# Bias terms as c·max(d, τ): one VectorE pass for each, summed by GpSimd and VectorE, with ScalarE taking the k, v and q copies

## The reference

```
hbias   = relu(dist[..., None] @ Wth + bth)        # 32 hidden values for each (query, key) pair
qs_bias = (hbias @ Wto + bto)[..., 0]
logits  = einsum('btnh,bfnh->bnft', k, q) + bias + qs_bias[:, None]
w       = softmax(logits)
```

## Time and profile before

| | |
|---|---|
| runs | 1380.3, 1382.73, 1384.69 us; median 1382.73 |
| profiled execution | 1388.81 us; its span, first to last instruction, 1387.1 us |
| groups 1 to 15's bias sums end | 125.1 to 1131.3 us |
| busy PE, DVE, ACT, POOL | 1228.3, 1222.8, 1064.8, 834.8 us |
| granted TensorE clock, mean | 0.970 |

### The profile page before, as it was taken

How to read it: one execution, slowest core, us unless ns; L and a number is a source line. 1 busy time by engine, 2 the same in 40 slices (tenths; PEclk the granted TensorE clock), 3 DMA queues, 4 the chain that set the end, 5 groups by cost and what they waited for, 6 DMA issues and landing times.

```text
span 1387.1 us, 39817 instructions
## 1 busy us (share of the span) xinstructions
PE 1228.3 (89%) x11184; PEld 1013.8 (73%) x11184; DVE 1222.8 (88%) x4922; ACT 1064.8 (77%) x3353; POOL 834.8 (60%) x889
## 2 busy tenths in 40 slices
PE   1599989898989899898989898989898999788897
PEld 1377878787878787777878787878787878666665
DVE  4899989898989999898989898989898988579996
ACT  4588878787878888787878686878787876568886
POOL 3677767676767677676767676767676754211110
PEclk9899999999999999999999999999999999989999
DMA  5201000002110000021100101111101000000000
GB/s 153 67 7 30 16 27 12 29 12 76 44 31 12 23 19 22 20 68 34 31 25 13 29 12 31 57 47 28 31 12 42 12 12 9 5 22 19 18 20 9
DMA packets 69117, 41.06 MB, mean 30 GB/s; under 512 B 14841, under 2 KB 63873, under 8 KB 68993
## 3 DMA queue, kind: packets, MB, share of 16 engines
q1 hardware_dynamic: 68992, 39.84, 10.1%
HBM read 23.29 MB, written 1.05 MB: 18 GB/s over the span
## 4 chain that ended last, share of the span: by engine, by line
issue 27%; DVE 24%; ACT 18%; PE 17%; POOL 3%; DVEq 1%; DMA 1%; ACTq 0%; SPq 0%; POOLq 0%
ACT prob L802 10%; DVE bias_acc L951 4%; PE M L582 3%; ACT relu_z L785 3%; PE O L552 3%; DVE score L998 3%; DVE qT L1123 3%; DVE hid L1073 3%; DVE st L1016 2%; PE M L628 2%; PE M L560 2%; PE L L689 1%; ACT probT L809 1%; ACT oT L814 1%; DVE rs L1025 1%
## 5 line engine op out<-in xcount | busy, mean ns | idle before, releaser
L802 ACT ACTIVATE prob<-score,nmax 128x128 f32<-128x128 f32 x1024 | 396.7, 390 | 182.7 <-DVE nmax L998 177.3
L1396 POOL TENSOR_TENSOR prob<-prob,rinv 128x512 f32<-128x512 f32 x256 | 293.9, 1148 | 234.0 <-DVE rinv L1006 231.9
L951 DVE SCALAR_TENSOR_TENSOR bias_acc<-relu_z,cst,bias_acc 128x512 f32<-128x512 f32 x370 | 339.7, 918 | 9.7 <-ACT relu_z L785 0.2
L785 ACT ACTIVATE relu_z<-dist_g,cst 128x512 f32<-128x512 f32 x386 | 294.9, 804 | 16.9 <-DMA cst<-cst_all 16.9
L998 DVE CUSTOM_DVE_ANT_0 score<-L,bias 128x128 f32<-128x128 f32 x1024 | 233.8, 282 | 4.2 <-PE L L528 1.5
L802 ACT ACTIVATION_READ_ACCUMULATOR prob<-score,nmax 128x1 f32 x1024 | 193.2, 189 | 0.0
L1391 POOL TENSOR_TENSOR sd<-mv,half 128x1 f32<-128x1 f32 x128 | 105.6, 825 | 120.4 <-DVE mv L1018 117.6
L538 PE MATMUL T<-ident,prob 128*128 128x128 f32 x1024 | 163.9, 284 | 4.7 <-POOL prob L1396 3.8
L552 PEld LDWEIGHTS O<-probT,v 128*64 128x64 f32 x2048 | 109.3, 136 | 62.0 <-issue 54.4
L582 PE MATMUL M<-wv,ctxT 128*128 128x512 f32 x256 | 147.0, 658 | 7.7 <-DVE hid L1073 5.1
L528 PE MATMUL L<-kT,qT 64*128 64x128 f32 x2048 | 149.6, 286 | 0.0
(11 more groups left out here) (134 smaller groups left out, 2226.7 us busy)
## 6 DMA issues: line engine op xcount, KB each, us to landing
dist_g<-in_fside_BxSxS SPq DMA_DIRECT2D x16, 256.0 KB, 2.7
mask_g<-in_mask_Bx1x1xS_ff SPq DMA_DIRECT2D x16, 256.0 KB, 3.5
ctxT<-ctxT_all SPq DMA_DIRECT2D x64, 64.0 KB, 1.9
xs<-x_all SPq DMA_DIRECT2D x64, 64.0 KB, 1.8
x_all<-xs SPq DMA_DIRECT2D x64, 64.0 KB, 1.9
wk<-in_L_xattn_Wk SPq DMA_DIRECT2D x4, 512.0 KB, 3.7
wv<-in_L_xattn_Wv SPq DMA_DIRECT2D x4, 512.0 KB, 4.3
wq<-in_L_xattn_Wq SPq DMA_DIRECT2D x4, 512.0 KB, 5.0
```

Source lines behind the costliest of these rows:

```text
L785: nc.scalar.activation(relu_z[:, z_slot(g, k), :], dist_g[:, :, :], ACT.Relu, bias=cst[:, C_BTH + k:C_BTH + k + 1], scale=cst[:, C_WTH + k ...
L802: last = nc.scalar.activation(prob[:, c, m, :], score[:, c, m, :], ACT.Exp, bias=nmax[:, c, m:m + 1], scale=-1.0, accum_out=rsum[:, c, m:m ...
L951: vec.scalar_tensor_tensor(out=bias_acc[:, :], in0=relu_z[:, z_slot(g, k), :], scalar=weight, in1=bias_acc[:, :], op0=ALU.mult, op1=ALU.ad ...
L1396: gp.tensor_tensor(prob[:, c, :, :], prob[:, c, :, :], rinv[:, c, :].rearrange("p (m o) -> p m o", o=1).broadcast_to([P, 4, P]), ALU.mult) ...
```

## The change

For Wth[k] not 0, relu(Wth·d + bth)·Wto is |Wth|·Wto·max(d, τ), with τ = -bth/Wth, plus a part that is linear in d. So a term is c·max(d, τ), one TENSOR_SCALAR with (max, mult), and all the linear parts together are a·1 + b·d, one TENSOR_SCALAR more.

For groups 1 to 15 (the bias of group 0 keeps the old form): DVE forms all 32 maxima into eight slots of `relu_z` (`maximum`) and begins `bias_acc` with a + b·d (`begin_sum`); POOL adds 20 of the 32 to `pool_acc`, with one instruction each (`add_term` of POOL), and its products and clamps go; DVE adds 12 to `bias_acc` as plain TENSOR_TENSORs. ACT's relus go, and ACT makes all six k, v, q copies of a unit. τ and c of all layers are computed once at the start by 23 small DVE instructions (`kinks`). SP loads one slice of constants for a group (`hst`) in place of three of `cst`.

The core of the diff (the first `add_term` is DVE's, the second POOL's):

```
+Z_SLOTS = 8
-Z_PLAN = plan([[1, 2, 2, 1, 0], [1, 2, 2, 1, 0], [1, 2, 2, 1, 0], [2, 2, 2, 0, 0]])
-TERM_PLAN = plan([[0, 2, 1, 1, 1], [1, 2, 1, 1, 1], [1, 2, 1, 1, 1], [1, 2, 2, 1, 1]])
+VEC_SLOTS = (1, 4, 6)
+VEC_TERMS = [k for k in range(BIAS_K) if k % Z_SLOTS in VEC_SLOTS]
+POOL_TERMS = [k for k in range(BIAS_K) if k % Z_SLOTS not in VEC_SLOTS]
+MAX_PLAN = plan([[0, 3, 2, 2, 1], [2, 2, 1, 2, 1], [2, 2, 1, 2, 1], [3, 3, 2, 0, 0]])
+VEC_ADD_PLAN = plan([[0, 0, 1, 1, 1], [0, 1, 1, 0, 1], [0, 1, 0, 1, 1], [1, 1, 1, 0, 0]])
+POOL_ADD_PLAN = plan([[0, 2, 2], [1, 2, 2], [1, 2, 2], [2, 2, 2]])
...
+            def maximum(g, k):
+                j = k - Z_SLOTS
...
+                vec.tensor_scalar(relu_z[:, k % Z_SLOTS, :], dist_g[:, :, :], hst[:, H_TAU + k:H_TAU + k + 1],
+                                  hst[:, H_C + k:H_C + k + 1], ALU.max, ALU.mult).then_inc(z_done, 1)
+            def begin_sum(g):
...
+                vec.tensor_scalar(bias_acc[:, :], dist_g[:, :, :], hst[:, H_B:H_B + 1], hst[:, H_A:H_A + 1], ALU.mult,
+                                  ALU.add).then_inc(term_done, 1)
+            def add_term(g, n):
...
+                vec.tensor_tensor(bias_acc[:, :], bias_acc[:, :], relu_z[:, k % Z_SLOTS, :], ALU.add).then_inc(term_done, 1)
...
             def terms(g, i, q):
...
+                    if i == 0 and q == 1:
+                        begin_sum(g + 1)
+                    for k in MAX_PLAN[i][q] if i < GROUP else ():
+                        maximum(g + 1, k)
+                    for n in VEC_ADD_PLAN[i][q] if i < GROUP else ():
+                        add_term(g + 1, n)
...
+            def add_term(g, n):
...
+                k = POOL_TERMS[n]
+                pool.wait_ge(z_done, z_count(g, k + 1))
...
+                gp.tensor_tensor(pool_acc[:, :, :], so_far[:, :, :], relu_z[:, k % Z_SLOTS, :].rearrange("p (b t) -> p b t", b=GROUP),
+                                 ALU.add).then_inc(pool_sum, 1)
...
-                if nxt:
-                    dve.wait_ge(v_done, after(g, i + 1, 2, 1))
-                    wait(dve, pv_done, after(g, i - 1, 2, 1))
-                    vec.tensor_copy(v[:, (i + 1) % 2, 512:1024], M0[:, :]).then_inc(v_kept[1], 1)
...
+                if nxt:
+                    act.wait_ge(v_done, after(g, i + 1, 2, 1))
+                    wait(act, pv_done, after(g, i - 1, 2, 1))
+                    nc.scalar.activation(v[:, (i + 1) % 2, 512:1024], M0[:, :], copy).then_inc(v_kept[1], 1)
```

More of the change, by code:

```diff
@@ L69, with z_count, wait, wait_first @@
 STATS_TERMS = (4, 8)
+def z_count(g, k):
+    return k if isinstance(g, int) and g == 0 else g * BIAS_K + (START_VEC_K - BIAS_K + k)
 def vec_count(g, k):
[L74 removed]
+    return k if isinstance(g, int) and g == 0 else g * (1 + VEC_ADDS) + (START_VEC_K - 1 - VEC_ADDS + k)
 def pool_count(g, k):
[L79 to L83 removed]
+    first = POOL_K - START_POOL_SKIP
+    return k - START_POOL_SKIP if isinstance(g, int) and g == 0 else g * POOL_ADDS + (first - POOL_ADDS + k)
 C_WTH, C_BTH, C_WTO = 0, BIAS_K, 2 * BIAS_K
 C_BTO = 3 * BIAS_K
[L89 to L90 removed]
+C_HI, C_LO, C_PW, C_PB, C_TAU, C_C = [C_BTO + 1 + n * BIAS_K for n in range(6)]
+C_A, C_B = C_C + BIAS_K, C_C + BIAS_K + 1
+C_ALL = C_B + 1
+H_TAU, H_C, H_A, H_B = [c - C_TAU for c in (C_TAU, C_C, C_A, C_B)]
+KINK_MAX = 1.0e38
+FLAT_BELOW = 1.0e-30
+E_HEADS = 16
+E_HD = 8
+EXPERTS = 8
+ROW_HEADS = 4
+F_GROUPS = BATCHES // GROUP
+VA = 32
+def wait(eng, sem, value):
+    if isinstance(value, int) and value < 1:
+        return
+    eng.wait_ge(sem, value)
+def wait_first(eng, consts, *counts):
+    pairs = [(s, v) for s, v in zip(counts[::2], counts[1::2]) if not isinstance(v, int) or v > 0]
+    pairs = [(s, v if isinstance(v, int) else eng.to_reg(v)) for s, v in pairs]
+    eng.wait_ge(consts, 3)
+    for s, v in pairs:
+        eng.wait_ge(s, v)
+def after(g, i, per, k=0):
+    return g * (GROUP * per) + (i * per + k + 1)
+CST_STEPS = 27
 E_HEADS = 16
@@ L831, in step @@
                     nc.scalar.activation(kT[:, (i + 1) % 2, 0:4, :], M0[:, :], copy).then_inc(k_kept[0], 1)
-                relus(g, i, 0)
+                relus(i, 0)
                 if cur:
                     exps(g, i, 0)
-                relus(g, i, 1)
+                relus(i, 1)
+                if nxt:
+                    act.wait_ge(k_done, after(g, i + 1, 2, 1))
+                    wait(act, qk_done, after(g, i - 1, 4, 3))
+                    nc.scalar.activation(kT[:, (i + 1) % 2, 4:8, :], M0[:, :], copy).then_inc(k_kept[1], 1)
                 if nxt:
@@ L853, in step @@
                     nc.scalar.activation(qT[:, (i + 1) % 2, 0:4, :], M0[:, :], copy, scale=HD ** -0.5).then_inc(q_kept[0], 1)
-                relus(g, i, 4)
+                    act.wait_ge(q_done, after(g, i + 1, 2, 1))
+                    nc.scalar.activation(qT[:, (i + 1) % 2, 4:8, :], M1[:, :], copy, scale=HD ** -0.5).then_inc(q_kept[1], 1)
+                relus(i, 4)
                 if cur:
@@ L1436, in step @@
                     for k in range(START_POOL_SKIP + POOL_FIRST, POOL_K):
-                        product(0, k)
-                        clamp(0, k)
-                        add(0, k)
+                        product(k)
+                        clamp(k)
+                        add(k)
                 if prev:
                     norm(g, i - 1, 3)
-                bias_too = 0 <= i < GROUP and there(g, GROUP)
+                adds = POOL_ADD_PLAN[i] if 0 <= i < GROUP and there(g, GROUP) else ((), (), ())
                 early = i in EARLY_STEPS and not there(g, GROUP)
```

206 lines of the change are left out of this document (123 added, 83 removed).

## The result

| | before | after |
|---|---|---|
| runs, median | 1383.71 us (4 runs, 1380.3 to 1386.45) | 1687.38 us (4 runs, 1686.49 to 1689.18) |
| ratio | | 1.2198, interval 1.2167 to 1.2229 |
| profiled execution, its span | 1388.81, 1387.1 us | 1689.18, 1687.3 us |
| bias sums of groups 0 and 15 start | 57.4, 1131.3 us | 57.9, 1431.3 us |
| a group | 71.6 us | 91.6 us |

(Between the sixteen bias sums lie fifteen intervals: 1373.4 / 15 = 91.6.) The kernel is 22% slower. All of it lies in the 15 groups: 1373.4 - 1073.9 = 299.5 us of the 300.4 between the profiled executions. The start, which got 23 instructions more, ends 0.5 us later, and the part behind the last bias sum went from 255.8 to 256.0 us.

What follows compares the result with a forecast made beforehand. DVE's in-order queue was taken to set the pace, PE nearly as full. Terms of -28.4, +23.6, +15.9, +1.3 and +6.9 summed to 19.3 us a group, +290 us over 15 groups: 1672 us, range 1485 to 1745.

Steps and rivals of the forecast that it cites:

- part 3: Turns at SBUF of DVE's maxima and adds with POOL's adds and norms: +15.9 us a group, bounds none to +43.
- part 4: DVE's wait for ACT's exponentials before inverse 2, formerly covered by the v copy: net +1.3 us a group.
- part 5: At q3, POOL's add before norm 2 awaits DVE's maximum, delaying the root that DVE's scale needs: +6.9 us a group.
- part 2: Work coming to DVE, timed alone: 32 maxima, one beginning and 12 adds, +23.6 us a group.
- The walk through the plans: Following a group's four steps by the instruction plans, POOL taken as always ready, to count DVE's blocked maxima and adds.
- A microsecond added to DVE is a microsecond of the group: DVE's in-order queue sets the pace, so a microsecond added to it in a group lengthens the group equally.
- part 1: Work leaving DVE: 23 STTs, the first term and 12 k, v, q copies, with overlaps and gaps counted: -28.4 us a group.
- Both are all but full: In a 71 us steady window DVE has 65.4 us of work and PE 66.3; ACT and POOL are not full.
- The other edits: ACT's extra room brings nothing; start and end together set at 0, with -5 to +6 us as bounds.
- the faster one: Rival: the one-input maxima pass beside POOL and only the 12 adds wait; 1338 us, chance 0.08.
- the rarer turns: Rival: POOL is usually late, so DVE's instructions wait on average as the STTs do; 1497 us, chance 0.13.
- no overlap: Rival: in the turns, the waiting instruction does nothing beforehand, so each blocked one costs more; 1760 us, chance 0.08.

Runs made afterwards that it cites:

- Experiment 2: The changed kernel with POOL's adds 2 to 20 of a group on 4 of 128 columns of each batch, rest left out: 1535.45 us.
- 11: The changed kernel with maxima over 4 of 512 columns, POOL's and DVE's adds keeping their size: 1529.62 us.
- 4: The changed kernel with maxima reading and writing the same elements in steps of 128: 1809.12 us.
- Experiment 1: The changed kernel with POOL's last add of steps 0 to 2 moved behind norm 2 and the root: 1603.33 us.
- Number 5: The kernel before with ACT taking the second halves of the k, v and q copies, its relus kept: 1400.33 us, ratio 1.0113.
- 7: The kernel before with the second k and q copies moved from DVE to ACT: 1396.82 us, ratio 1.0090.
- 9: 6 plus eight one-column memsets at the start of DVE's code and the tile they write: 1379.29 us, ratio 0.9952 against the kernel before.
- number 8: Experiment 1 plus one POOL add of steps 1, 2 and 3 moved from before norm 1 to before norm 0: 1595.43 us.
- 10: The changed kernel with the edits of Experiment 1 and Experiment 2 together: 1479.24 us.
- 6: The kernel before with only the second k copy moved from DVE to ACT: 1430.54 us, ratio 1.0322.
- 12: The kernel before with 123 one-column memsets at the start on DVE and the tile they write: 1387.08 us, ratio 1.0003.

## Why the prediction was right

The forecast was 1672 us, with 1485 to 1745; measured 1687.38. The terms, a group:

| step of the prediction | forecast us | measured us | from |
|---|---|---|---|
| parts 1 to 3, work of DVE | +11.1 | +10.4 | DVE busy, (1379.3 - 1222.8) / 15 |
| of these, part 3 alone | +15.9 | +14.9 | (25.7 + 15.3 + 0.7) - 45 x 0.07 - 23.6 |
| part 4, exponentials | +1.3 | +2.3 | (49.2 - 15.4) / 15 |
| part 5, root | +6.9 | +7.1 | (111.8 - 5.8) / 15 |
| `hid` behind PE | 0 | +0.7 | (17.0 - 6.1) / 15 |
| not assigned | 0 | -0.5 | |
| sum | 19.3 | 20.0 | |

(25.7 is 32 maxima of 804 ns, 15.3 the 12 adds, 0.7 the one `begin_sum`; 23.6 is part 2. The -0.5 is what is left of the group's 20.0 when the rest is taken off.)

The total came nearer than its terms, and that is in part luck: parts 1 to 3 were 0.7 us a group too high, part 4 was 1.0 too low and `hid` was put at nothing, and these nearly cancel. Two of the three mechanisms behind the total (parts 3 and 5) are each borne out by experiments; part 4 is only sized by its row.

- **Part 3 was right in kind and 1 us too high in size.** It counted 8 blocked maxima a group and one half-covered, and 8 blocked adds; the trace has 9.9 and 7.0. Experiment 2 shows most of the excess going with POOL's adds, 11 that the wait doesn't depend on the maximum's own size, and 4 that a slower form of the maximum doesn't escape it. One of the signs missed: POOL's adds were to be 1.27 us at the median and up to 1.8, and are 1.44 and up to 2.10. POOL pays for the turns too, which the sum had only through the root. The walk through the plans had one place the other way round: at q3 of step 0, DVE's add was to wait for POOL's. It was next in DVE's queue when POOL's add got its maximum, went first (at 899.11), and POOL paid, the 2.02 us above.
- **Part 5 was right, wait by wait but for one.** The forecast had 1.7, 2.95, 1.7 and 0.75 us for the four steps; the trace has 2.66, 2.65, 1.44 and 0.66, the same in nearly every group. Step 0 is the odd one: the turn that DVE's add did not wait for came back as root wait. Experiment 1 takes all but 0.8 us a group of it away.
- **Part 4 was 1 us low.** It reckoned with the v copy's 0.6 us a step; the exponentials come later against DVE's work once copies are gone. Number 5 points the same way (73.6 us against 15.4), though there ACT also has more work, since it keeps its relus.
- **PE's wait for norm 2 was not in the prediction.** It is 8 us a group on PE, in the same stretch in which DVE waits for the root. What it costs apart from that wait no run tells, since experiment 1 takes both away; the 29 us that 1 gave back beyond its forecast may be its share.
- **"A microsecond added to DVE is a microsecond of the group" gave the right total, but no run tests it.** The busy time of an engine and its waits always add up to the time, so the table checks the sizes of the terms and not the rule. The other half of it, which the prediction implies in part 1, did not hold: numbers 5, 7 and 9 take 4 to 12 copies a group off DVE and gain at most 0.5%, with the unexplained gaps at the loop's jump (below) in 5 and 7. Nor did it in the changed kernel: number 8 takes 3.0 us a group off DVE's records and the group falls by 0.8. "Both are all but full" was the right reading, and "DVE's queue sets the pace" was half of it. That the -28.4 us of part 1 counted in full is, as we read it, because parts 2 and 3 filled the room again.
- **The other edits at nothing** held: ACT's room brought nothing, start and end moved by under 1 us.
- Of the rivals, the faster one fell with the maxima's 804 ns mean, the rarer turns with the DVE adds' median of 1466, no overlap with a run of 1687 and not 1760 us and with blocked maxima of 1509 ns at most.

The rule of the Trainium skill (SBUF — State Buffer, section "SBUF: two separate sides"), that the engine which comes second "fully blocks", is borne out by experiment 11 as to who waits, and in that the wait is the same for a short instruction as for a long one: 1.08 us at worst over the shortest for four columns, 1.00 for 512. The price stays under its letter in both: 1327 ns at worst and not 0.25 + 1.27 = 1.52 us, 1509 and not 0.51 + 1.27 = 1.78.

The split of the 20.0 us by the experiments: without the wait for norm 2 and the root (1) 5.7 less, without the turns with POOL's adds (2) 10.2 less, without both (10) 13.9 less. The effects overlap by 2.0, about the root wait that number 2 takes off as well ((111.8 - 80.9) / 15 = 2.1). The 6.1 left goes by the waits in 10 with the turns with norms, the exponentials and PE; nothing here removed these. What TensorE's lower clock has in the 20.0 is not separated.

## What to carry to other kernels

Work that moves from DVE to GpSimd while both read and write SBUF has to be priced with the turns: every 1.26 us add of GpSimd cost a ready DVE instruction about 1.0 us. What the help is worth then hangs on where it stands: the same 19 adds were worth nothing in the order of the change, and 91 us with norm 2 and the root ahead of the last of them in a step. Before an instruction goes into a shared helper's queue, look at what stands behind it: one add in each of three steps of a group waited for a late input and held back a 1.04 us norm for PE and a root for DVE, and its new place alone gave 84 us. And where two engines are within a few per cent of full, price an edit by both: here load taken off one of them brought hardly anything.

## What the runs showed of the hardware that was not expected

**The clock of TensorE fell as its gaps grew.** In the kernel before, the granted clock in a group is near 0.5 in one stretch only, behind the jump of the loop. After, it is there three times in a group; two are behind such gaps as this one. Rows of some windows, of before and then of after (columns as above):

```profile
702.00:705.40 3.40, 3.12 (x14) 3.13 (x15) 2.88 (x16) 1.29 (x7) 2.54 (x3) 0.54 0.11 32
705.40:708.80 3.40, 3.40 (x31) 2.47 (x30) 3.40 (x14) 2.07 (x5) 2.32 (x3) 0.96 0.00 0
```

```profile
895.30:898.70 3.40, 1.15 (x18) 0.98 (x18) 2.63 (x17) 3.35 (x15) 0.00 (x0) 1.00 0.00 0
898.70:902.10 3.40, 0.56 (x7) 0.21 (x4) 1.09 (x3) 1.28 (x6) 3.20 (x3) 0.51 0.00 0
902.10:905.50 3.40, 3.40 (x17) 3.07 (x19) 2.58 (x9) 1.20 (x2) 1.35 (x4) 0.50 0.00 0
905.50:908.90 3.40, 2.69 (x32) 2.50 (x29) 3.33 (x15) 0.00 (x0) 2.48 (x3) 0.99 0.01 2
```

PE was busy 1.15 and 0.56 of two times 3.4 us, while POOL first waited for its maximum (until 898.90) and then worked off add and norm 2. The clock went to its lower level (1.2 GHz of 2.4), and PE did 17 matmuls in 3.4 us at it, 32 in 2.69 when it had risen. With it PE's busy time rose from 66.3 to 70.7 us a group with the same matmuls, which fits the mean clock in these windows, 0.98 and 0.91. What it adds to the time was not measured by itself; the clock is higher in the experiments that take waits away (0.891 in the change, 0.922 in 1, 0.935 in 2, 0.943 in 10), though in 8 it is 0.913, under number 1's.

**Eight instructions that do nothing were worth 51 us.** Numbers 6 and 9 differ only in memsets that run once at the start and in the tile that they write, and the wait at the loop's jump is up to 5.2 us in one and 2.6 in the other. In 5 and 7 a second such wait turned up, up to 1.0 us at `nmax` in 5 and up to 1.9 at `h` in 7:

```profile
DVE rinv L1012 <- issue: 37.6, 13, 3.0
DVE h L1037 <- issue: 21.9, 13, 1.9
```

So a change of DVE's code by a few instructions can move the time by 3% through something that is not in the edit. That it is the place of the code in memory is a guess that fits 6 and 9; the one test of a rule for it, 12, did not confirm it, and the place of the tiles in SBUF is a rival that no run excludes for number 6. How fast the numbers 5 and 7 would be at another place was not tried: the two waits of 7 are 59.5 us in all, 27 more than the 32.4 of the kernel before, and without these 27 it would lie near 1370, by this estimate 1% under the kernel before. So what moving the copies is worth stays open; k's alone gained 0.5%.
